# Attention scores stored block behind block, and the maximum over them taken in two halves, in a two-layer graph kernel

## The chip, the cores and the metric

The kernel runs on one core of one Trainium2 chip. The time is that of the device, in microseconds (us). The kernel before took 818.03 us, the median of 3 runs that lay between 816.57 and 819.36 us. Engines are named as in the profile: PE is TensorE's matmul, PEld its weight load, DVE is VectorE, ACT is ScalarE, POOL is GpSimd and SP is SyncE.

## The reference, cut to what matters

A graph has 3125 nodes with 128 features and 103,125 edges. The first layer adds to each node a weighted sum over its neighbours. The second layer, where the change lies, is attention over the edges that arrive at each node:

```
h = relu(layernorm(x))
q, k, v = h @ Wq + bq, h @ Wk + bk, h @ Wv + bv
logits = sum(q[dst] * k[src], axis=-1) / sqrt(128)
m = segment_max(logits, dst);  ex = exp(logits - m[dst])
alpha = ex / segment_sum(ex, dst)[dst]
x = x + elu(segment_sum(alpha * v[src], dst) + h @ Ws + bs)
```

## The kernel before

The kernel turns edges into dense tables. Nodes are laid out in NT = 25 tiles of P = 128. The first stage (up to about 70 us) sorts out windows of edges; the second (to about 472 us) builds, for each tile of destination nodes, a table `gt` of the logarithms of edge counts and the weighted sums of the first layer; the third (to about 508 us) makes keys `kT`, queries `qT`, values `vals` and the skip term. The fourth is attention, one step for each of the 25 tiles t of destinations, written in queues that run in order, one for each engine.

In a step, a tile of 128 destinations is scored against all 25 source blocks of 128 nodes. The score table `sm[:, v, :]` has the source node within its block on the partitions; along a partition lie all blocks h and, in each, the 128 destinations d. A ring of RING = 4 such tables is in use (v is t modulo 4), and as many tables `gl_sb` of edge logarithms, which SP loads four tiles ahead. The blocks are taken in NSG = 4 groups given by `SG`: 6, 6, 6 and 8 blocks, the last of which holds 7 real blocks and one of padding (NTP = 26), filled once by POOL with a very low number. Groups 0 and 2 share one pair of PSUM banks, groups 1 and 3 the other, so group 2 can be scored only after group 0 is read out, and group 0 of tile t+1 only after group 2 of tile t.

For one group the work goes round the engines: ACT seeds the banks from `gl_sb` (`seed`, L668, a large number where there is no edge; it waits until DVE has read the group that was there); PE adds the scores (`scores`, L1259, one float32 matmul for each block, which the profile shows as two records); DVE subtracts them from `gl_sb` into `sm` (`mask`, L994). After the fourth group DVE takes the maximum over the 25 blocks and the pad for each partition and destination (L1033), PE turns the result (L1280), DVE reduces it to one maximum for each destination and puts it on a diagonal (L1010, L1013), PE spreads it with a matmul against ones (L1286), ACT copies it to `mbc` (L710), POOL subtracts it from the four groups of `sm` (`subtract_max`, L493), ACT takes the exponential of each (L717), and PE multiplies by the values and a column of ones (`values`, L1270, 129 columns, again two records for each block, with `sm` as the stationary operand). Then DVE and ACT normalise and apply the skip term and the ELU (L1017 to L1026, L691 to L696), and POOL adds the residual.

The steps overlap. In step t PE does, in this order: turn the maximum of t-1 (L1280); scores of t, group 2; spread the maximum of t-1 (L1286); scores of t, group 3; values of t-2, groups 0 and 1; scores of t+1, groups 0 and 1; values of t-2, groups 2 and 3. DVE does: mask 0, mask 1; L1010, L1013 for t-1; L1017, L1020 for t-3; mask 2; L1026 for t-3; mask 3; the maximum. ACT does: seeds 2 and 3 of t; `mbc` of t-1; exponential 0 of t-1, seed 0 of t+1, exponential 1, seed 1 of t+1, exponential 2, the ELU of t-3, exponential 3.

The layout of `sm` before is paired: two neighbouring blocks i = 0, 1 are interleaved word by word, so word 2d + i of pair k belongs to block 2k + i and destination d. The function `twos` gives that view. `mask` writes with a step of 2 words, L1033 reads for each d the two words of a pair, hops 256 words to the next pair, and so on 13 times, and `values` loads its weights with a step of 2 words.

Of the kernel before, what the change touches and what calls it, by code (L numbers as in the profile page):

```python
# [79 lines left out]

SG = [(0, 6), (6, 6), (12, 6), (18, 8)]
NTP = NT + 1
NSG = len(SG)
# [3 lines left out]
STEPS = NT + 3  # L87
assert sum(n for _, n in SG) == NTP and all(n % 2 == 0 for _, n in SG) and NSG % 2 == 0 and LOOP_TO < NT

# [8 lines left out]
def build_gnn(nc, x, dst, dst_next, dst_far, dst_rows, samples, src, edge_weight, ids, consts, slow_iota,  # L98
              ws_t, wn_t, wq, wk, wv, wskip, b_s, b_n, bq, bk, bv, b_skip, out):
    outer = ExitStack()  # L100
    with outer:
# [3 lines left out]
        def sb(stack, name, shape, dt=F32):  # L105
            return stack.enter_context(nc.sbuf_tensor(name, shape, dt))
# [10 lines left out]
        def ps(i):  # L117
            return bank[i // 2][:, i % 2, :]
# [162 lines left out]
        s4 = ExitStack()  # L281
        mx = sb(s4, "mx", [P, P])
        mcol = sb(s4, "mcol", [P, 1])
        diag = sb(s4, "diag", [P, P])
# [5 lines left out]
        res = sb(s4, "res", [P, 2, D])  # L290
        sm = sb(s4, "sm", [P, RING, NTP * P])
        gl_sb = sb(s4, "gl_sb", [P, RING, NTP * P])
        s4.close()
        s34.close()
        gl = [sem(f"gl{k}") for k in range(RING)]
        seeded, primed, pad_ready = sem("seeded"), sem("primed"), sem("pad_ready")
        s_ready, masked, mx_ready, mt_ready, m_ready, dg_ready, mb_ready, mbc_ready = (
# [12 lines left out]

        def twos(v, a, n):

            return sm[:, v, a * P:(a + n) * P].rearrange("p (k d i) -> p k d i", d=P, i=2)

# [119 lines left out]
        def _(pool):  # L434
# [47 lines left out]
            pool.memset(vals[:, :, D:D + 1], 1.0)  # L482
            pool.memset(gl_sb[:, :, NT * P:NTP * P], -FLOOR).then_inc(pad_ready, 1)
            for d in range(1, NC):
# [3 lines left out]
            def subtract_max(t, v):  # L488
                pool.wait_ge(mbc_ready, 1 + t + 1)
                for a, n in SG:  # L490
                    part = twos(v, a, n)
                    top = mbc[:, v % 2, :].unsqueeze(1).unsqueeze(3).to_broadcast([P, n // 2, P, 2])
                    pool.tensor_tensor(part, part, top, ALU.subtract).then_inc(sub_done, 1)  # L493
# [240 lines left out]
        def _(dve):  # L734
# [256 lines left out]
            def mask(t, v, g):  # L991
                a, n = SG[g]
                dve.wait_ge(s_ready, t * NSG + g + 1)
                V.tensor_tensor(twos(v, a, n).rearrange("p k d i -> p k i d"),  # L994
                                gl_sb[:, v, a * P:(a + n) * P].rearrange("p (k i d) -> p k i d", d=P, i=2),
                                score_bank(g)[:, 0:n * P].rearrange("p (k i d) -> p k i d", d=P, i=2),
                                ALU.subtract).then_inc(masked, 1)

            def dve_step(t, v, turn):
# [18 lines left out]
                if three:  # L1018
                    dve.wait_ge(rd_ready, 2 * (t - 3) + 1)
                    V.reciprocal(rden[:, u3, :], rden[:, u3, :]).then_inc(rd_ready, 1)  # L1020
                if now:
                    mask(t, v, 2)
                if three:
# [7 lines left out]
                if now:  # L1031
                    dve.wait_ge(masked, 2 + (t + 1) * NSG)
                    V.tensor_reduce(mx[:], twos(v, 0, NTP).rearrange("p k d i -> p d k i"), AXY, ALU.max).then_inc(mx_ready, 1)  # L1033

            dve.wait_ge(pad_ready, 1)
            for t in range(LOOP_FROM):
# [9 lines left out]
        def _(pe):  # L1046
# [216 lines left out]
            def values(t, v, g):  # L1263
# [4 lines left out]
                for h in range(a, min(a + n, NT)):  # L1268
                    weights = twos(v, h - h % 2, 2).rearrange("p k d i -> p (k d) i")[:, :, h % 2]
                    ins = T.matmul(ps(4 + v % 2)[:, 0:D + 1], weights, vals[:, h, :], start=h == 0,  # L1270
                                   stop=h == NT - 1)
# [85 lines left out]
```

## Time and profile before

| | us |
|---|---|
| median of 3 runs | 818.03 |
| the profiled execution | 822.52 |
| its span, first to last instruction | 820.6 |
| PE busy, whole span | 735.8 |
| DVE busy | 618.0 |
| ACT busy | 526.4 |
| POOL busy | 253.9 |

Busy time is that in which at least one instruction of the engine was running. The granted TensorE clock was 0.99 of full speed over the span. The table is over the whole kernel; only the last 310 us, the attention, are touched by the change, so the shares of that stretch matter and are among the rows below.

### The profile page before, as it was taken

How to read it: one execution, taken by the hardware profiler on the slowest of the kernel's cores; microseconds unless marked ns; L12 is line 12 of the kernel's file. 1: busy time of each engine (PE TensorE's matmuls, PEld its weight loads, DVE VectorE, ACT ScalarE, POOL GpSimd, SP SyncE). 2: the span in 40 equal slices, each digit the busy share in tenths (PEclk: the TensorE clock that was granted, in tenths of full speed). 3: DMA queues.
4: the chain of work that ended last, by engine and by line, in shares of the span. 5: the costliest groups of instructions: out<-in, count | busy, mean ns of one | idle time of the engine just before them, and what ended most of it. 6: DMA issues, size and time to landing. Idle time of an engine off the chain costs nothing.

```text
span 820.6 us, 24234 instructions
## 1 busy us (share of the span) xinstructions
PE 735.8 (90%) x9625; PEld 719.5 (88%) x9625; DVE 618.0 (75%) x778; ACT 526.4 (64%) x1056; POOL 253.9 (31%) x206
## 2 busy tenths in 40 slices
PE   0147999999999999999999688699999999999997
PEld 0147999999999999999999666699999999999996
DVE  6767779889889889889885653776777677767771
ACT  4949857667667767767766234566676666667654
POOL 4636000000000000000000141366676667666766
PEclk9999999999999999999999979999999999999999
DMA  9831223212212212212312170404334433443300
GB/s 263 256 103 77 88 81 133 111 80 120 120 80 120 120 80 117 122 80 110 130 80 115 51 320 1 161 2 168 120 133 163 165 114 136 166 161 106 148 8 12
DMA packets 17667, 96.79 MB, mean 118 GB/s; under 512 B 2482, under 2 KB 8860, under 8 KB 11100
## 3 DMA queue, kind: packets, MB, share of 16 engines
q1 hardware_dynamic: 14572, 90.08, 28.9%
q0 software_dynamic: 3056, 6.17, 2.9%
q8 instruction: 27, 0.44, 0.2%
q14 instruction: 12, 0.10, 0.0%
HBM read 51.62 MB, written 44.63 MB: 117 GB/s over the span
## 4 chain that ended last, share of the span: by engine, by line
PE 83%; ACT 6%; DVE 5%; issue 2%; POOL 1%; another core or an unknown queue 1%; DMA 1%; POOLq 1%; PEld 0%; PEldq 0%; ACTq 0%; DVEq 0%
PE bank L1270 18%; PE bank L1119 17%; PE bank L1259 16%; PE bank L1136 9%; PE bank L1134 9%; PE bank L1101 8%; PE bank L1225 1%; PE bank L1230 1%; ACT kT L554 1%; ACT wst L607 1%; DVE oh_key L914 1%; ACT gst L605 1%; PE bank L1087 1%; DVE junk L751 1%
## 5 line engine op out<-in xcount | busy, mean ns | idle before, releaser
L493 POOL TENSOR_TENSOR sm<-sm,mbc 128x768 f32<-128x768 f32 x100 | 174.5, 1777 | 115.4 <-ACT mbc L710 115.4
L1134 PE MATMUL bank<-oh_key,oh_lo 128*128 128x100 bf16 x1600 | 170.6, 208 | 8.0 <-ACT wst L607 6.7
L1136 PE MATMUL bank<-oh_key,oh_lo 128*128 128x50 bf16 x3200 | 170.9, 187 | 0.0
L1134 PEld LDWEIGHTS bank<-oh_key,oh_lo 128*128 128x128 bf16 x1600 | 155.7, 97 | 10.5 <-ACT wst L607 8.6
L1136 PEld LDWEIGHTS bank<-oh_key,oh_lo 128*128 128x128 bf16 x3200 | 163.8, 97 | 0.9
L1259 PE MATMUL bank<-qT,kT 128*128 (+1 forms) x1250 | 154.1, 277 | 6.8 <-ACT bank L668 6.8
L1270 PE MATMUL bank<-vals,sm 128*128 128x129 f32 x1250 | 154.8, 281 | 0.0
L1259 PEld LDWEIGHTS bank<-qT,kT 128*128 128x128 f32 x1250 | 147.1, 194 | 8.2 <-ACT bank L668 7.0
L1270 PEld LDWEIGHTS bank<-vals,sm 128*128 128x128 f32 x1250 | 150.9, 196 | 0.0
L914 DVE TENSOR_TENSOR oh_key<-oh_key,xt 128x1600 bf16<-128x1600 bf16 x150 | 141.9, 1001 | 0.0
L605 ACT ACTIVATE gst<-bank,tiny_col 128x400 f32<-128x400 f32 x200 | 122.4, 612 | 23.6 <-PE bank L1136 20.4
L476 POOL TENSOR_TENSOR xn<-xs,ln_c 128x640 f32<-128x640 f32 x5 | 7.8, 1564 | 405.1 <-DVE ln_c L874 405.1
L1119 PE MATMUL bank<-hv,qT 128*128 (+1 forms) x650 | 128.3, 285 | 2.0 <-DVE kT L844 2.0
L717 ACT ACTIVATE sm<-sm 128x768 f32<-128x768 f32 x100 | 89.9, 899 | 58.5 <-POOL sm L493 55.5
L994 DVE TENSOR_TENSOR sm<-gl_sb,bank 128x768 f32<-128x768 f32 x100 | 100.0, 1020 | 32.6 <-PE bank L1259 32.6
L1119 PE MATMUL bank<-hv,wsb 128*128 (+1 forms) x600 | 116.0, 275 | 0.0
L909 DVE TENSOR_TENSOR oh_lo<-xt,lo_tab 128x4096 bf16<-128x4096 bf16 x50 | 114.2, 2285 | 0.0
L607 ACT COPY wst<-bank 128x400 f32<-128x400 f32 x200 | 100.7, 504 | 0.0
L1119 PEld LDWEIGHTS bank<-hv,qT 128*128 128x128 f32 x650 | 96.7, 191 | 2.5 <-DVE kT L844 2.3
L1033 DVE TENSOR_REDUCE mx<-sm 128x128 f32<-128x3328 f32 x25 | 90.5, 3620 | 0.9
L1119 PEld LDWEIGHTS bank<-hv,wsb 128*128 128x128 f32 x600 | 91.1, 192 | 0.0
L844 DVE TENSOR_TENSOR kT<-kT,bank 128x512 f32<-128x512 f32 (+1 forms) x84 | 52.7, 628 | 49.3 <-PE bank L1119 48.3
(122 smaller groups left out, 808.3 us busy)
## 6 DMA issues: line engine op xcount, KB each, us to landing
gt<-gst SPq DMA_DIRECT2D x25, 1600.0 KB, 5.5
gl_sb<-gt SPq DMA_DIRECT2D x25, 1600.0 KB, 6.7
records<-rec SPq DMA_DIRECT2D x1, 2015.0 KB
out<-res SPq DMA_DIRECT2D x24, 64.0 KB, 1.5
src_i<-in_src SPq DMA_DIRECT2D x1, 403.0 KB, 6.2
w_in<-in_edge_weight SPq DMA_DIRECT2D x1, 403.0 KB, 6.6
dst_i<-in_dst SPq DMA_DIRECT2D x1, 403.0 KB, 7.1
dstn_i<-in_dst_next SPq DMA_DIRECT2D x1, 403.0 KB, 7.2
```

Of the source, the lines that this page charges most:

```text
L493: pool.tensor_tensor(part, part, top, ALU.subtract).then_inc(sub_done, 1)
L605: nc.scalar.activation(place, counts, ACT.Ln, bias=tiny_col[:, 0:1], scale=EULER).then_inc(evacs, 1)
L607: nc.scalar.copy(sums, cells[:, :, KEYS:2 * KEYS]).then_inc(evacs, 1)
L909: V.tensor_tensor(oh_lo[:, u, :, :, :], along(F_LO, P), table(lo_tab, P), ALU.is_equal).then_inc(onehot, 1)
L914: V.tensor_tensor(block(1 + w), block(0), along(F_W + w, KEYS), ALU.mult).then_inc(onehot, 1)
L994: V.tensor_tensor(twos(v, a, n).rearrange("p k d i -> p k i d"), gl_sb[:, v, a * P:(a + n) * P].rearrange("p (k i d) -> p k i d", d=P, i=2 ...
L1033: V.tensor_reduce(mx[:], twos(v, 0, NTP).rearrange("p k d i -> p d k i"), AXY, ALU.max).then_inc(mx_ready, 1)
L1119: ins = T.matmul(to, wsb[w][:, cols], hv[:, bass.ds(s, 1), :].rearrange("p t f -> p (t f)"), start=n == 0 and not first, stop=n == len(par ...
L1134: T.matmul(cells, lo, oh_key[:, u, m, 0:2 * KEYS, i], start=True, stop=False, skip_group_check=True)
L1136: ins = T.matmul(cells[:, KEYS:2 * KEYS], lo, oh_key[:, u, m, (1 + w) * KEYS:(2 + w) * KEYS, i], start=False, stop=w == 2, skip_group_chec ...
L1259: ins = T.matmul(score_bank(g)[:, j * P:(j + 1) * P], kT[:, (a + j) * P:(a + j + 1) * P], qT[:, bass.ds(t * P, P)], start=False, stop=True ...
L1270: ins = T.matmul(ps(4 + v % 2)[:, 0:D + 1], weights, vals[:, h, :], start=h == 0, stop=h == NT - 1)
```

## The change

`sm` loses the pairing: block h lies whole behind block h-1, `sm[:, v, h*128 + d]`. The pad block goes, with its fill and the wait for it. The groups become 7, 6, 6 and 6 blocks. `mask` writes contiguously, `subtract_max` has the same elements in a view of blocks, and `values` loads contiguous weights. The one maximum over 26 blocks becomes one over the 13 blocks of groups 0 and 1, issued on DVE ahead of mask 2; one over the 12 blocks of groups 2 and 3, after mask 3; and an elementwise maximum of the two results. Both halves read, for each destination d, one word of each block with a hop of 128 words between them.

```
-SG = [(0, 6), (6, 6), (12, 6), (18, 8)]
-NTP = NT + 1
+SG = [(0, 7), (7, 6), (13, 6), (19, 6)]
+HALF = SG[2][0]
...
-        sm = sb(s4, "sm", [P, RING, NTP * P])
-        gl_sb = sb(s4, "gl_sb", [P, RING, NTP * P])
+        mx_half = sb(s4, "mx_half", [P, 2, P])
+        sm = sb(s4, "sm", [P, RING, NT * P])
+        gl_sb = sb(s4, "gl_sb", [P, RING, NT * P])
...
-            return sm[:, v, a * P:(a + n) * P].rearrange("p (k d i) -> p k d i", d=P, i=2)
+            return sm[:, v, a * P:(a + n) * P].rearrange("p (h d) -> p h d", d=P)
...
-            pool.memset(gl_sb[:, :, NT * P:NTP * P], -FLOOR).then_inc(pad_ready, 1)
...
-                    part = twos(v, a, n)
-                    top = mbc[:, v % 2, :].unsqueeze(1).unsqueeze(3).to_broadcast([P, n // 2, P, 2])
+                    part = blocks(v, a, n)
+                    top = mbc[:, v % 2:v % 2 + 1, :].to_broadcast([P, n, P])
...
-                V.tensor_tensor(twos(v, a, n).rearrange("p k d i -> p k i d"),
-                                gl_sb[:, v, a * P:(a + n) * P].rearrange("p (k i d) -> p k i d", d=P, i=2),
-                                score_bank(g)[:, 0:n * P].rearrange("p (k i d) -> p k i d", d=P, i=2),
+                V.tensor_tensor(sm[:, v, a * P:(a + n) * P], gl_sb[:, v, a * P:(a + n) * P], score_bank(g)[:, 0:n * P],
                                 ALU.subtract).then_inc(masked, 1)
+            def half_max(t, v, k):
+                a, n = (HALF, NT - HALF) if k else (0, HALF)
+                dve.wait_ge(masked, 2 + t * NSG + 2 * k + 2)
+                V.tensor_reduce(mx_half[:, k, :], blocks(v, a, n).rearrange("p h d -> p d h"), AX, ALU.max).then_inc(mx_part, 1)
...
                     V.reciprocal(rden[:, u3, :], rden[:, u3, :]).then_inc(rd_ready, 1)
                 if now:
+                    half_max(t, v, 0)
                     mask(t, v, 2)
...
                 if now:
-                    dve.wait_ge(masked, 2 + (t + 1) * NSG)
-                    V.tensor_reduce(mx[:], twos(v, 0, NTP).rearrange("p k d i -> p d k i"), AXY, ALU.max).then_inc(mx_ready, 1)
+                    half_max(t, v, 1)
+                    dve.wait_ge(mx_part, 2 * t + 2)
+                    V.tensor_tensor(mx[:], mx_half[:, 0, :], mx_half[:, 1, :], ALU.max).then_inc(mx_ready, 1)
...
-                    weights = twos(v, h - h % 2, 2).rearrange("p k d i -> p (k d) i")[:, :, h % 2]
-                    ins = T.matmul(ps(4 + v % 2)[:, 0:D + 1], weights, vals[:, h, :], start=h == 0,
+                    ins = T.matmul(ps(4 + v % 2)[:, 0:D + 1], sm[:, v, h * P:(h + 1) * P], vals[:, h, :], start=h == 0,
```

## Rows read from the trace of the kernel before

**Rows 1.** Busy by engine, 21 steady steps: PE, PEld, DVE, ACT, POOL, clock, DMA.
```profile
545.19:793.13 247.94, 247.94 (x2165) 247.94 (x2164) 180.66 (x210) 162.11 (x273) 165.03 (x126) 1.00 0.37 131
```

**Rows 2.** Timeline of PE over one steady step: start us, length us, line, count.
```profile
651.14 0.27 PE L1280 MATMUL bank<-ident,mx 128*128 128x128 f32 x1
...
657.21 2.84 PE L1259 MATMUL bank<-qT,kT 128*128 x24
659.88 3.23 PE L1270 MATMUL bank<-vals,sm 128*128 128x129 f32 x26
662.95 0.27 PE L1280 MATMUL bank<-ident,mx 128*128 128x128 f32 x1
```

**Rows 3.** Timeline of DVE, the same step; in brackets idle time and its releaser.
```profile
651.45 0.29 DVE L1010 TENSOR_REDUCE mcol<-bank 128x1 f32<-128x128 f32 x1 [2.07 <-PE bank L1280]
...
652.17 0.16 DVE L1020 RECIPROCAL rden<-rden 128x1 f32<-128x1 f32 x1
652.79 0.95 DVE L994 TENSOR_TENSOR sm<-gl_sb,bank 128x768 f32<-128x768 f32 x1 [0.46 <-PE bank L1259]
653.66 0.35 DVE L1026 SCALAR_TENSOR_TENSOR pre<-bank,rden,hT 128x128 f32<-128x128 f32 x1
654.58 1.22 DVE L994 TENSOR_TENSOR sm<-gl_sb,bank 128x1024 f32<-128x1024 f32 x1 [0.57 <-PE bank L1259]
655.84 3.62 DVE L1033 TENSOR_REDUCE mx<-sm 128x128 f32<-128x3328 f32 x1
```

**Rows 4.** Timeline of POOL and ACT, the same step.
```profile
653.36 6.97 POOL L493 TENSOR_TENSOR sm<-sm,mbc 128x768 f32<-128x768 f32 x4 [3.69 <-ACT mbc L710]
...
655.04 0.85 ACT L717 ACTIVATE sm<-sm 128x768 f32<-128x768 f32 x1 [1.76 <-POOL sm L493]
655.79 0.80 ACT L668 ACTIVATE bank<-gl_sb 128x768 f32<-128x768 f32 x1
```

**Rows 5.** Groups by form, attention stage: busy us, mean ns of one, idle before.
```profile
L493 POOL TENSOR_TENSOR sm<-sm,mbc 128x768 f32<-128x768 f32 x75 | 121.9, 1654 | 115.4 <-ACT mbc L710 115.4
...
L493 POOL TENSOR_TENSOR sm<-sm,mbc 128x1024 f32<-128x1024 f32 x25 | 53.6, 2146 | 0.0
...
L717 ACT ACTIVATE sm<-sm 128x1024 f32<-128x1024 f32 x25 | 26.5, 1060 | 9.7 <-POOL sm L493 9.7
L668 ACT ACTIVATE bank<-gl_sb 128x896 f32<-128x896 f32 x25 | 22.6, 904 | 0.7 <-DVE sm L994 0.6
```

**Rows 6.** Groups by form, DVE, first 70 us.
```profile
L827 DVE TENSOR_TENSOR xin<-win,nid 128x384 bf16<-128x384 f32 x3 | 2.5, 849 | 0.0
L785 DVE TENSOR_TENSOR rec<-rest,part_b 128x806 f32<-128x806 f32 x1 | 1.6, 1627 | 0.0
L827 DVE TENSOR_TENSOR xin<-win,nid 128x256 bf16<-128x256 f32 x2 | 1.3, 632 | 0.8 <-issue 0.8
L780 DVE TENSOR_TENSOR rest<-w_in,part_b 128x806 f32<-128x806 f32 x1 | 1.0, 1000 | 0.0
```

**Rows 7.** Timeline of PE, a run of transposes in the second stage.
```profile
303.37 1.06 PE L1101 MATMUL bank<-ident,wst 128*128 128x128 f32 x8
```

**Rows 8.** Timeline of all engines, the first attention step.
```profile
510.18 0.96 DVE L994 TENSOR_TENSOR sm<-gl_sb,bank 128x768 f32<-128x768 f32 x1 [2.79 <-PE bank L1259]
511.23 0.81 ACT L668 ACTIVATE bank<-gl_sb 128x768 f32<-128x768 f32 x1 [2.17 <-DVE sm L994]
...
512.09 3.18 PE L1259 MATMUL bank<-qT,kT 128*128 128x128 f32 x26 [0.71 <-ACT bank L668]
...
513.74 0.95 DVE L994 TENSOR_TENSOR sm<-gl_sb,bank 128x768 f32<-128x768 f32 x1 [1.36 <-PE bank L1259]
...
516.56 3.62 DVE L1033 TENSOR_REDUCE mx<-sm 128x128 f32<-128x3328 f32 x1
```

**Rows 9.** Timeline of all engines, around the last maximum.
```profile
796.26 1.23 DVE L994 TENSOR_TENSOR sm<-gl_sb,bank 128x1024 f32<-128x1024 f32 x1 [0.57 <-PE bank L1259]
...
801.95 0.27 PE L1280 MATMUL bank<-ident,mx 128*128 128x128 f32 x1
```

More of the change, by code:

```diff
@@ L87 @@
 STEPS = NT + 3
-assert sum(n for _, n in SG) == NTP and all(n % 2 == 0 for _, n in SG) and NSG % 2 == 0 and LOOP_TO < NT
+assert sum(n for _, n in SG) == NT and NSG % 2 == 0 and LOOP_TO < NT
 TG = [(a, min(4, NT - a)) for a in range(0, NT, 4)]
@@ L295, in build_gnn @@
         gl = [sem(f"gl{k}") for k in range(RING)]
-        seeded, primed, pad_ready = sem("seeded"), sem("primed"), sem("pad_ready")
+        seeded, primed, mx_part = sem("seeded"), sem("primed"), sem("mx_part")
         s_ready, masked, mx_ready, mt_ready, m_ready, dg_ready, mb_ready, mbc_ready = (
@@ L309, in score_bank, with blocks @@
             return bank[g % 2][:].rearrange("p a b -> p (a b)")
-        def twos(v, a, n):
-            return sm[:, v, a * P:(a + n) * P].rearrange("p (k d i) -> p k d i", d=P, i=2)
+        def blocks(v, a, n):
+            return sm[:, v, a * P:(a + n) * P].rearrange("p (h d) -> p h d", d=P)
         def live(t):
@@ L1031, in dve_step @@
                 if now:
-                    dve.wait_ge(masked, 2 + (t + 1) * NSG)
-                    V.tensor_reduce(mx[:], twos(v, 0, NTP).rearrange("p k d i -> p d k i"), AXY, ALU.max).then_inc(mx_ready, 1)
-            dve.wait_ge(pad_ready, 1)
+                    half_max(t, v, 1)
+                    dve.wait_ge(mx_part, 2 * t + 2)
+                    V.tensor_tensor(mx[:], mx_half[:, 0, :], mx_half[:, 1, :], ALU.max).then_inc(mx_ready, 1)
             for t in range(LOOP_FROM):
```

## The prediction

> **What bounds the kernel now.** I read the page first for the whole span: PE is busy 735.8 of 820.6 us. I then cut the attention stage out with busy time by stretch [rows 1]: over 247.94 us, PE is busy for 247.94, at a granted clock of 1.00 (the 2.4 GHz level), while DVE is busy for 180.7, ACT 162.1 and POOL 165.0. That stretch is 21 steps of 247.94 / 21 = 11.81 us, as the distance of two L1280 in the timeline also says [rows 2]. So a step ends when PE has gone through its 50 score records, 50 value records and 3 others; nothing that only makes DVE, ACT or POOL faster shortens it, and whatever makes PE wait lengthens it one for one.
>
> The timelines of the other engines say how far each is from making PE wait. I count from the start of a step, T = 651.14 [rows 2]. DVE ends its maximum at 655.84 + 3.62 = T+8.32 [rows 3], and PE asks for it at T+11.81: 3.5 us of slack. The near one is another wait. PE starts the scores of t+1, group 0, at 657.21 = T+6.07 [rows 2]. These need seed 0, which runs on ACT from 655.79 to 656.59 [rows 4], and that needs mask 2, over at 652.79 + 0.95 = T+2.60 [rows 3]. Today ACT is at that seed late only because exponential 0 stands ahead of it.
>
> **The change part by part.** First the pitch of PE. Groups 7, 6, 6, 6 make the same 25 blocks. Scores come every (659.88 - 657.21) / 24 = 0.111 us, values every (662.95 - 659.88) / 26 = 0.118 [rows 2]. Is the difference of 0.0065 the step of 2 words in the weights, or the 129th column and what comes with it? Rows on both sides: transposes whose stationary operand is read every 25th word come at (1.06 - 0.28) / 7 = 0.112 [rows 7], so a hop in the stationary operand by itself costs nothing there; that is nearest in kind, and I take 0. The other end is 50 x 0.0065 = 0.32 us gained a step.
>
> Masks: 768 elements take 0.95 and 1024 take 1.22 [rows 3], so 128 elements take 0.135, already the slope of one element each 1.05 ns; contiguous writes have no more to give. Mask 0 becomes 1.09, mask 3 0.95. The pad's fill ran once, beside other work: 0.
>
> Next the maximum. Now 3328 elements take 3.62 us [rows 3], 1.04 ns each and 0.15 fixed; the hops of 256 words between pairs are free. In the change every element hops. The trace before has no such reduction. Bounds: below, the present 1.04 ns. Above, the DVE rows of the first 70 us with a hop each element: L827 reads every fifth word, 384 in 849 ns and 256 in 632; less 150 fixed that is 1.82 and 1.88 ns (by their difference alone 1.70); L785 writes every fifth word, 806 in 1627 ns against 1000 for the contiguous L780, 0.78 ns more each, 1.82 in all [rows 6]. I take 1.81, the long read. The first half is then 0.15 + 1664 x 0.00181 = 3.17 us, the second 0.15 + 1536 x 0.00181 = 2.93, and the joining operation 0.29 like other 128-column ones (L1010) [rows 3]: 6.39 for 3.62.
>
> [...]
>
> Second, where it stands. The first half sits on DVE ahead of mask 2, behind L1020, which starts at 652.17 = T+1.03 [rows 3]; the half starts at T+1.11, and queued behind it are mask 2, L1026 and mask 3. Neighbours on DVE overlap by 0.08 (652.79 + 0.95 against 653.66). Mask 2 runs from 1.11 + 3.17 - 0.08 = T+4.20 to T+5.15, 2.55 later than today. ACT takes up a seed 0.09 after the mask (510.18 + 0.96 to 511.23) and PE its scores 0.05 after the seed, with about 0.11 more for the first weight load that then isn't hidden [rows 8]. A seed of 896 is 0.90 [rows 5]. So the scores of t+1 start at 5.15 + 0.09 + 0.90 + 0.16 = T+6.30. PE is free for them at T+6.07, plus 0.01 (two score records fewer, two value records more ahead of them). It waits 0.22 us in each step. The rest of the step is unchanged, 11.81 becomes 12.03, and 21 steps give +4.6 us.
>
> Beside it stands the way through POOL and ACT to the same seed: the subtraction of 7 blocks is (2146 - 1654) / 2 = 246 ns longer [rows 5], so exponential 0 starts at 655.04 + 0.25 [rows 4]; the seed follows 0.75 later and 0.11 more for the longer exponential (1060 against 850 for two blocks [rows 4, 5]), at T+5.01. That is 0.23 ahead of DVE's way; with a fast reduction this one would be last, and scores could start at 5.01 + 0.90 + 0.16 = T+6.07: no wait, but no slack either.
>
> The rest of DVE's step: L1026 and mask 3 to T+6.27, second half from 6.31 to 9.24, the joining from 9.28 to 9.57. PE wants it at T+12: hidden, at less cover. Masks 0 and 1 follow to T+11.45, 0.9 before the next L1010. Seed 1 waits for mask 3 and exponential 1 and ends near T+7.6, before its scores at 7.9. SP's loads wait for mask 3 and have whole steps to spare; POOL's and SP's queues are moved past nothing.
>
> Two ends don't repeat. In the first step mask 2 starts at 513.74 with DVE idle 1.36 before it [rows 8]. The first half begins there near 512.6 and ends at 515.8; mask 2, mask 3 (0.95 each), 2.93 and 0.29 bring the maximum to 520.8 instead of 516.56 + 3.62 = 520.2, and the next step's seed, with no values yet to cover it, loses about as much again: +0.9 (0.3 to 1.3). In the last step T is 793.13 - 0.31 = 792.82 (the L1010 that ends rows 1's stretch), so the last maximum is there at 792.82 + 9.57 = 802.4 where PE now turns it at 801.95 [rows 9], and everything after waits for it: +0.5.
>
> **Sum.** 4.6 + 0.9 + 0.5 = +6.0 us, made against the profiled 822.52 (span 820.6 and 1.9 around it): 828.5. The profiled execution is 0.5% above the median of 818.03; nothing of the sum hangs on that, so I add the same 6.0 to the median: 824.0.
>
> **Rivals.**
>
> A dearer hop. If a hop of 128 words costs twice the extra of five words, it is 1.04 + 2 x 0.77 = 2.6 ns. Then DVE itself is the bound: its fixed parts in a step (from L1010 to the first half 0.80; mask 2, L1026, mask 3 and handovers 2.1; the two 0.15 less overlaps; joining 0.2; masks 0 and 1 1.9) are 5.3, and with 3200 elements the step is 5.3 + 8.3 = 13.6 us: +1.8 x 21 = 38 us, about 857. It decides from 2.04 ns on. For it: a longer hop. Against it: no row here shows more than 1.88, and the pair hop of 256 words is free. [...]
>
> The hop is free. L1033 hops between pairs at no cost, and only two-input operations show the penalty in rows 6. The halves cost 1.88 and 1.75, DVE gets slack, and PE waits by POOL's way for nothing: 818.0, no change. It decides below 1.70 ns, where the wait is gone.
>
> The paired weights are what slows the values. Then every step gives back 0.32. With the hop as I forecast, PE is at the scores 0.17 sooner, but they start at T+6.30 all the same; only the 24 records behind give 0.16, so a step is +0.07, the ends +1.4 less 150 x 0.0065 = 1.0: +1.9 us, 820, within what can't be told.
>
> The other side: paired weights and a free hop together. This is one mechanism, the interleaving taken off PE, with price 0.32 a step, and it decides if the values' pitch drops to 0.112. POOL's way holds the scores at T+6.07, so only 0.16 of it is kept: 3.4 us, and 1.0 in the last 150 records: 813.6, faster. For it: the pitch difference of 0.0065, of which one more column explains little. Against it: rows 7, and rows 6 speak against the free hop.
>
> That the change doesn't do what it says: if L1020 were late for want of values of t-3, the half would be too; rows 3 show it at T+1.03, with no idle time, so no.
>
> **How the numbers follow.** My forecast, 0.50; dearer hop, 0.12; free hop, 0.16; paired weights with a dear hop, 0.14; both gone, 0.08. A measurement of this kernel tells about 0.3%, 2.5 us, from no change. Slower: the forecast but for its low edge (by 1.70 ns it gives +1.7 us), the dearer hop, and a little of the third: 0.58. Same: 0.28. Faster: 0.14. The likeliest case's own range is 819.7 to 827. To hold the time 8 times in 10 the range goes down to 815, which takes in the free hop, and up to 834; the dearer hop is left out above.
>
> **What would show it.** In the profile after: the 13-block reduction near 3.17 us and the 12-block one near 2.93; mask 2 without idle time before it, starting 4.2 us after L1280; idle time of PE at L1259, released by L668, about 0.2 us and 21 times; a step of 12.03; L1270's pitch still 0.118. The prediction is wrong if the halves are near 1.9 or above 3.6 us, or if L1270's pitch falls to 0.112.

## The result, and the profile after

The changed kernel takes 823.24 us (median of 6 runs, 820.73 to 824.61) against 817.30 for the kernel before (6 runs, 816.42 to 820.20): 5.9 us more, a ratio of 1.0063 with a 95% interval of 1.0044 to 1.0082. The forecast was 824.0, slower. The direction and the size came out; the way to them did so only in part. That the total came so near is luck: the steps cost less than forecast and the ends more, and within a step two errors cancel in part.

The profiled execution took 824.57 us. I first cut out the same 21 steps. The columns are as in [rows 1], from the third L1283 (the former L1280) to the twenty-fourth; [rows 1] begins and ends 0.31 us later in its step, at L1010.

```profile
542.40:793.30 250.90, 247.18 (x2165) 243.19 (x2164) 236.61 (x252) 163.17 (x274) 175.61 (x126) 1.00 0.37 130
```

PE isn't saturated any more: 3.7 of 250.9 us are idle, and PEld, in which a wait shows better, idles for 7.7. DVE has gone from 180.7 to 236.6 us. A step is 250.9 / 21 = 11.95 us. Next the costliest groups by form, attention stage (busy us, mean ns, idle before):

```profile
L1273 PE MATMUL bank<-vals,sm 128*128 128x129 f32 x1250 | 148.8, 276 | 0.0
L1263 PEld LDWEIGHTS bank<-qT,kT 128*128 128x128 f32 x1250 | 148.4, 195 | 18.4 <-ACT bank L668 9.7 <-issue 8.7
...
L493 POOL TENSOR_TENSOR sm<-sm,mbc 128x768 f32<-128x768 f32 x75 | 134.7, 1829 | 0.0
...
L1000 DVE TENSOR_REDUCE mx_half<-sm 128x128 f32<-128x1664 f32 x25 | 76.8, 3072 | 0.0
L1000 DVE TENSOR_REDUCE mx_half<-sm 128x128 f32<-128x1536 f32 x25 | 73.0, 2918 | 0.9
...
L493 POOL TENSOR_TENSOR sm<-sm,mbc 128x896 f32<-128x896 f32 x25 | 52.3, 2092 | 110.4 <-ACT mbc L710 110.4
...
L1038 DVE TENSOR_TENSOR mx<-mx_half 128x128 f32<-128x128 f32 x25 | 16.9, 674 | 0.9
```

The halves are 3.07 and 2.92 us (forecast 3.17 and 2.93). Two rows nobody asked for: POOL takes 1.83 us for the 768 elements that took 1.65 [rows 5], and the joining takes 0.67 where 0.29 was summed. The timeline of one steady step (T = 650.09, the L1283 that begins it) has the rest, all engines:

```profile
650.09 0.27 PE L1283 MATMUL bank<-ident,mx 128*128 128x128 f32 x1
...
652.31 7.44 POOL L493 TENSOR_TENSOR sm<-sm,mbc 128x896 f32<-128x896 f32 x4 [3.39 <-ACT mbc L710]
...
654.21 0.94 DVE L994 TENSOR_TENSOR sm<-gl_sb,bank 128x768 f32<-128x768 f32 x1
654.43 0.95 ACT L717 ACTIVATE sm<-sm 128x896 f32<-128x896 f32 x1 [2.20 <-POOL sm L493]
...
655.29 0.90 ACT L668 ACTIVATE bank<-gl_sb 128x896 f32<-128x896 f32 x1
...
656.33 2.98 PEld L1263 LDWEIGHTS bank<-qT,kT 128*128 128x128 f32 x26 [0.35 <-issue]
656.33 3.16 PE L1263 MATMUL bank<-qT,kT 128*128 x26 [0.16 <-ACT bank L668]
...
659.27 0.63 DVE L1038 TENSOR_TENSOR mx<-mx_half 128x128 f32<-128x128 f32 x1
659.33 2.84 PE L1273 MATMUL bank<-vals,sm 128*128 128x129 f32 x24
...
662.01 0.27 PE L1283 MATMUL bank<-ident,mx 128*128 128x128 f32 x1
```

Three things are to be seen. The 24 value records go from 659.33 to 662.01: 2.68 / 24 = 0.112 us each, not 0.118 as in [rows 2]. PE stands before the scores of group 0, for seed 0, as forecast. But seed 0 starts at 655.29, the moment exponential 0 gives ACT free; mask 2 had been done since 655.15, 0.14 before. What came last was POOL's way, not mask 2, though not by much: a seed follows its mask by some 0.04 us where it waits for nothing else (the run with the hop and POOL's old view, below), so 0.10 of the 0.14 counts. This step takes 11.92 us. Three in four do; the fourth, in which seed 0 comes some 0.1 us later, takes 12.0 to 12.1, and the mean is 11.95.

The wait is sized by the step: 103 records at 0.1115 would be 11.48, so PE waits 0.46 us in each on the mean, where I had 0.22 on top of 11.81.

The three stretches of attention, from the first instruction of the third stage (L977 on DVE, at 472.72 and 466.67 us) in both profiles:

| | before | after | forecast |
|---|---|---|---|
| to the third L1010 (L1013) | 72.5 | 76.0 | +0.9 |
| 21 steps | 247.9 | 250.9 | +4.6 |
| from there to the end | 27.5 | 29.2 | +0.5 |
| sum | 347.9 | 356.1 | +6.0 |

The sum is 8.2 us, more than the 5.9 of the medians. What lies ahead of attention differs by 6 us between profiles, even of one and the same design, so I compare stretches, not spans. Those 6 us go with the chip: the runs below that were made on the chip where the kernel before takes 818.3 us have 466.3 to 466.9 there, like the profile of after; those made on the three chips where it takes 824.2 to 824.6 have 471.8 to 472.9, like the profile of before. What it is in the chip, no run here shows. The profile of before, with 822.52 us, is thus to be held against 824 and not 818: it is of an execution some 1.7 to 2.1 us faster than the median, while that of after lies 1.3 above its own. Together that covers the 2.3 us between 8.2 and 5.9.

So the ends cost 5.2 us by the two profiles and, by the medians, 5.9 less the 3.0 of the steps, 2.9; forecast were 1.4. Busy time by stretch, three of after and then three of before: its first and third lie at the same place in the program as those of after, its second is the one in which its clock was low (columns as above; the granted clock is the number behind the brackets):

```profile
509.00:515.00 6.00, 3.80 (x21) 3.61 (x20) 5.66 (x5) 1.68 (x2) 0.00 (x0) 0.74 0.40 130
527.00:533.00 6.00, 4.29 (x22) 4.11 (x23) 5.96 (x7) 2.70 (x4) 0.23 (x1) 0.72 0.27 113
804.00:810.00 6.00, 5.80 (x37) 5.80 (x38) 0.73 (x4) 2.06 (x3) 4.93 (x3) 0.72 0.04 11
```

```profile
515.00:521.00 6.00, 3.81 (x28) 3.04 (x26) 5.66 (x4) 1.41 (x2) 0.00 (x0) 1.00 0.55 190
527.00:533.00 6.00, 4.68 (x25) 4.44 (x25) 5.07 (x3) 4.62 (x6) 4.24 (x3) 0.72 0.76 273
804.00:810.00 6.00, 6.00 (x53) 6.00 (x52) 0.42 (x3) 2.84 (x6) 6.00 (x4) 1.00 0.01 3
```

In each of the three stretches of after the granted clock is 0.72 to 0.74 on the mean, a mixture of the 2.4 GHz and the 1.2 GHz level; before has one such stretch. Each costs at most 6 x 0.28 = 1.7 us; in the last one PE is busy nearly throughout and does 37 records in 6 us, where before does 53. They follow idle time of PE: in after PE had stood 2.2 us before 511.78 for a seed that stood behind the first half maximum, and 1.8 us around the last L1283 and L1289. Not all idle time was followed by one: PE also stood 3.04 us before 523.44, and its clock was 1.00 from 523 to 529. From the timeline of after:

```profile
506.82 3.03 DVE L1000 TENSOR_REDUCE mx_half<-sm 128x128 f32<-128x1664 f32 x1
...
509.77 1.81 DVE L994 TENSOR_TENSOR sm<-gl_sb,bank 128x768 f32<-128x768 f32 x2
510.81 1.68 ACT L668 ACTIVATE bank<-gl_sb 128x896 f32<-128x896 f32 x2 [3.11 <-DVE sm L994]
...
511.78 4.80 PE L1263 MATMUL bank<-qT,kT 128*128 128x128 f32 x26 [2.20 <-ACT bank L668]
514.43 0.29 DVE L1038 TENSOR_TENSOR mx<-mx_half 128x128 f32<-128x128 f32 x1
...
516.42 0.27 PE L1283 MATMUL bank<-ident,mx 128*128 128x128 f32 x1
...
803.17 0.33 PE L1283 MATMUL bank<-ident,mx 128*128 128x128 f32 x1 [1.11 <-DVE mx L1038]
...
804.20 0.49 PE L1289 MATMUL bank<-diag,ones 128*128 128x128 f32 x2 [0.71 <-DVE diag L1016]
```

The first maximum is there at 514.43 + 0.29 = 514.72, 48.05 us after the start of the third stage, against 47.46 before: the 0.6 later that I had forecast. But PE turns it only at 516.42, 2.2 us later than before, since its 26 records from 511.78 take 4.80 us where 26 take 3.18 at full clock [rows 8]; that is 1.6 of the 2.2.

Two such stretches more are up to 3.4 of the 8.2 us. How many an execution has isn't set by the kernel alone. On one chip (that of the late-join run below) the kernel before took 814.8 to 816.5 us in the nine executions with a mean granted clock of 0.990 or 0.991, and 818.1 to 820.3 in the fourteen with 0.984 to 0.988. So what one profile shows at the two ends is good to a few microseconds only, while the steady steps, at a clock of 1.00, are not touched by it.

### The profile page after: what moved, and what is told of

Same layout as the page of the kernel before. It is cut to its first block, busy times and chain, and to the rows that moved or that the text cites. A ratio compares the mean times of both kernels' runs of the same rounds, so it can differ in the third digit from the quotient of the medians.

```text
span 822.8 us, 24313 instructions
## 1 busy us (share of the span) xinstructions
PE 737.6 (90%) x9625; PEld 717.1 (87%) x9625; DVE 686.0 (83%) x828; ACT 527.1 (64%) x1056; POOL 267.8 (33%) x205
## 4 chain that ended last, share of the span: by engine, by line
PE 51%; POOL 20%; issue 14%; ACT 6%; DVE 6%; POOLq 1%; DMA 1%; PEld 0%; PEldq 0%; ACTq 0%; DVEq 0%
POOL sm L493 18%; PE bank L1123 17%; PE bank L1140 9%; PE bank L1138 9%; PE bank L1105 8%; PE bank L1273 2%; PE bank L1229 1%; PE bank L1263 1%; POOL res L499 1%; PE bank L1234 1%; ACT kT L554 1%; ACT wst L607 1%; ACT gst L605 1%; PE bank L1091 1%; DVE junk L751 1%
## 5 line engine op out<-in xcount | busy, mean ns | idle before, releaser
L493 POOL TENSOR_TENSOR sm<-sm,mbc 128x896 f32<-128x896 f32 (+1 forms) x100 | 186.0, 1894 | 110.4 <-ACT mbc L710 110.4
L1263 PE MATMUL bank<-qT,kT 128*128 (+1 forms) x1250 | 157.6, 281 | 13.1 <-ACT bank L668 13.0
L1000 DVE TENSOR_REDUCE mx_half<-sm 128x128 f32<-128x1664 f32 (+1 forms) x50 | 149.8, 2995 | 0.9
L1273 PE MATMUL bank<-vals,sm 128*128 128x129 f32 x1250 | 148.8, 276 | 0.0
L1273 PEld LDWEIGHTS bank<-vals,sm 128*128 128x128 f32 x1250 | 145.0, 193 | 0.0
L717 ACT ACTIVATE sm<-sm 128x896 f32<-128x896 f32 (+1 forms) x100 | 87.1, 871 | 65.2 <-POOL sm L493 64.6
L994 DVE TENSOR_TENSOR sm<-gl_sb,bank 128x896 f32<-128x896 f32 (+1 forms) x100 | 95.9, 977 | 5.3 <-PE bank L1263 4.9
L668 ACT ACTIVATE bank<-gl_sb 128x896 f32<-128x896 f32 (+1 forms) x100 | 83.1, 833 | 20.4 <-DVE sm L994 17.9
```

What stands on the lines that cost most here:

```text
L994: V.tensor_tensor(sm[:, v, a * P:(a + n) * P], gl_sb[:, v, a * P:(a + n) * P], score_bank(g)[:, 0:n * P], ALU.subtract).then_inc(masked, 1)
L1000: V.tensor_reduce(mx_half[:, k, :], blocks(v, a, n).rearrange("p h d -> p d h"), AX, ALU.max).then_inc(mx_part, 1)
L1263: ins = T.matmul(score_bank(g)[:, j * P:(j + 1) * P], kT[:, (a + j) * P:(a + j + 1) * P], qT[:, bass.ds(t * P, P)], start=False, stop=True ...
L1273: ins = T.matmul(ps(4 + v % 2)[:, 0:D + 1], sm[:, v, h * P:(h + 1) * P], vals[:, h, :], start=h == 0, stop=h == NT - 1)
```

## Experiments

Twelve kernels, each timed beside the kernel before on the same chip. Step, start and end are read as in the table above, from each profile; for the ends, what was just said of single profiles holds. Ratios are to the kernel before, with 95% intervals. The edits shown are cut to the lines that matter; the runs whose text speaks of a tiny scale also have `scale=2.0 ** -100` in the exponential. What holds for before and after: step 11.81 and 11.95, start 72.5 and 76.0, end 27.5 and 29.2.

**Is it the paired weights that slow the values?**

```
-                    weights = twos(v, h - h % 2, 2).rearrange("p k d i -> p (k d) i")[:, :, h % 2]
+                    weights = sm[:, v, h * P:(h + 1) * P]
```

> The kernel before, in which the value matmuls load 128 neighbouring words as weights (those of block h as if the table were not paired) and not every second word; the products are therefore of mixed-up scores, nothing else differs. Theory A, the step of 2 words in the weights slows the value matmuls: a value record comes every 0.1115 us and not 0.118, no wait of PE appears (seed 0 ends at T+5.45 and PE is there at T+5.92), a steady step is 11.48 us and not 11.81, the time some 8 us lower, 809. Rival, the pitch belongs to the 129th column or to where the values lie, and fell in the changed kernel for another reason: pitch 0.118, step 11.81, 817.

Measured: ratio 0.9916 (0.9892 to 0.9939), step 11.51, start 71.8, end 26.4. From its timeline of PE:

```profile
655.55 3.07 PE L1270 MATMUL bank<-vals,sm 128*128 128x129 f32 x26
658.46 0.27 PE L1280 MATMUL bank<-ident,mx 128*128 128x128 f32 x1
```

The 26 records take 2.91 us, 0.112 each: nothing but the step of the weights was changed, and 0.30 us a step went. Theory A stands. The reverse, the changed kernel with paired weights:

```
-                    ins = T.matmul(ps(4 + v % 2)[:, 0:D + 1], sm[:, v, h * P:(h + 1) * P], vals[:, h, :], start=h == 0,
+                    b = min(h - (h - a) % 2, a + n - 2)
+                    weights = sm[:, v, b * P:(b + 2) * P].rearrange("p (d i) -> p d i", i=2)[:, :, (h - a) % 2]
+                    ins = T.matmul(ps(4 + v % 2)[:, 0:D + 1], weights, vals[:, h, :], start=h == 0,
```

> The changed kernel in which the value matmuls load every second word of two neighbouring blocks as weights, as the kernel before did (the products are of mixed-up scores). This is the kernel that the prediction summed. A value record comes every 0.118 us again. Scores of group 0 start at T+6.24, where POOL's way puts them, as in the changed kernel; only the 24 value records behind them are dearer: a step of 11.95 + 0.16 = 12.10 us, 3.3 us more in the steady steps, the ends 0.5 to 1 more, the time 0.5% above that of the changed kernel on the same chip. Rival, the pitch of the values comes from elsewhere: step 11.95.

Measured: ratio 1.0082 (1.0057 to 1.0106), step 12.09, start 76.2, end 28.1. The step is the expected one to 0.01; the total, whose interval reaches over that of the changed kernel, can't tell 0.2% from the expected 0.5%. Its values, from the timeline of PE:

```profile
660.34 2.99 PE L1275 MATMUL bank<-vals,sm 128*128 128x129 f32 x24
663.17 0.27 PE L1285 MATMUL bank<-ident,mx 128*128 128x128 f32 x1
```

2.83 / 24 = 0.118. So the step that I had summed as 12.03 is 12.09 in a kernel with the pitch that I had assumed.

**Why is POOL slower?**

```
-                    part = twos(v, a, n)
-                    top = mbc[:, v % 2, :].unsqueeze(1).unsqueeze(3).to_broadcast([P, n // 2, P, 2])
+                    part = sm[:, v, a * P:(a + n) * P].rearrange("p (h d) -> p h d", d=P)
+                    top = mbc[:, v % 2:v % 2 + 1, :].to_broadcast([P, n, P])
```

> The kernel before, in which POOL's subtraction of the maximum takes the view of the changed kernel (blocks one behind the other, the row of maxima repeated for each block), which pairs wrong maxima with the scores; the exponential has a tiny scale so that its results stay finite. Theory B, it is this view that makes POOL slower: 768 elements take 1.83 us and not 1.65, with the paired reduction on DVE as before; exponential 0 starts 0.18 later, still no wait of PE, time 817 to 818. Rival, POOL is slowed by DVE's hopping reads at the same time: 1.65 us stays.

Measured: ratio 1.0041 (1.0026 to 1.0056), step 11.98, start 73.2, end 27.3. Groups by form:

```profile
L493 POOL TENSOR_TENSOR sm<-sm,mbc 128x768 f32<-128x768 f32 x75 | 134.5, 1821 | 102.4 <-ACT mbc L710 102.4
...
L493 POOL TENSOR_TENSOR sm<-sm,mbc 128x1024 f32<-128x1024 f32 x25 | 59.4, 2378 | 0.0
```

Theory B stands: with the paired maximum on DVE, POOL is slower all the same, by the view alone. Where two neighbouring elements share a word of the second operand, an element costs (2146 - 1654) / 256 = 1.92 ns [rows 5], else (2378 - 1821) / 256 = 2.18. (The changed kernel's own rows give (2092 - 1829) / 128 = 2.05.) The total missed: I had looked at seed 0 only. The timeline of ACT and PE in this run:

```profile
656.90 0.84 ACT L717 ACTIVATE sm<-sm 128x768 f32<-128x768 f32 x1 [1.92 <-POOL sm L493]
657.65 0.80 ACT L668 ACTIVATE bank<-gl_sb 128x768 f32<-128x768 f32 x1
658.68 0.84 ACT L717 ACTIVATE sm<-sm 128x768 f32<-128x768 f32 x1 [0.24 <-POOL sm L493]
...
658.90 1.28 PE L1259 MATMUL bank<-qT,kT 128*128 x10
659.43 0.80 ACT L668 ACTIVATE bank<-gl_sb 128x768 f32<-128x768 f32 x1
```

ACT waits 0.24 us for POOL's second subtraction, and seed 1 behind it ends at 660.23; PE, through with group 0 after 12 records at 658.90 + 1.34 = 660.24, can't take it up before 660.23 + 0.16. That is about 0.15 of the 0.17 us a step. There is a second narrow place, seed 1.

**What does the hop cost in time, and which way binds?**

```
-  blocks(v, a, n).rearrange("p h d -> p d h")
+  sm[:, v, a * P:(a + n) * P].rearrange("p (d h) -> p d h", d=P)
```

> The changed kernel, in which both half maxima read the same number of words without a hop (for each destination 13 or 12 neighbouring words, which are the wrong ones; the exponential has a tiny scale for the same reason as before). The halves take 1.88 and 1.75 us and mask 2 starts near T+2.9. Theory C, in the changed kernel seed 0 waits for POOL's first subtraction and exponential 0, and mask 2 comes only just before them: exponential 0 still starts near T+4.3, PE still waits some 0.2 us, a steady step is 11.9 and not 11.95; the time falls by 1 us in the steady steps and by 2 to 3 at the two ends, to 820. Rival, the prediction's own step (mask 2 sets the start, POOL is only slowed by DVE's hops): POOL back at 1.9 for the first group, step 11.78 or less, 817.

Measured: ratio 0.9987 (0.9971 to 1.0003), step 11.93, start 71.5, end 26.4. From its timeline:

```profile
652.70 1.89 DVE L1000 TENSOR_REDUCE mx_half<-sm 128x128 f32<-128x1664 f32 x1
...
655.90 0.95 ACT L717 ACTIVATE sm<-sm 128x896 f32<-128x896 f32 x1 [2.19 <-POOL sm L493]
...
656.76 0.90 ACT L668 ACTIVATE bank<-gl_sb 128x896 f32<-128x896 f32 x1
...
657.80 3.16 PE L1263 MATMUL bank<-qT,kT 128*128 x26 [0.15 <-ACT bank L668]
```

Without the hop the first half takes 1.89 us for 3.07, and the steady step gains 0.02 us. Theory C stands: exponential 0 and seed 0 start where POOL lets them, and PE's wait is there still. Without the hop the two ends lose their cost, though: 4.5 us at the start and 2.8 at the end against the profile of after. The ratio fell by 0.0076 against the changed kernel, some 6 us (good to 2), of which the steps are 0.3, and more than the 3 us expected. The hop's price is paid at the ends.

With POOL's old kind of view as well:

```
-  part = blocks(v, a, n)
+  part = sm[:, v, a * P:(a + n) * P].rearrange("p (h e i) -> p h e i", e=P // 2, i=2)
-  top = mbc[:, v % 2:v % 2 + 1, :].to_broadcast([P, n, P])
+  top = mbc[:, v % 2, 0:P // 2].unsqueeze(1).unsqueeze(3).to_broadcast([P, n, P // 2, 2])
```

> As the run before, and besides POOL's subtraction with a view like that of the kernel before (two neighbouring words share a maximum, the wrong one). Theories B and C together: POOL's first subtraction takes 1.90 us and not 2.10, exponential 0 starts near T+4.15, PE waits some 0.1 us or less, a step is 11.7 to 11.78, the time 2.5 to 4 us below that of the run before. If C is wrong, no difference to the run before.

Measured: ratio 0.9926 (0.9907 to 0.9946), step 11.74, start 70.7, end 26.2. As expected: 0.20 us a step, by POOL's view, once mask 2 is early; the time fell by some 5 us against the run before, more than the 4 expected. And that view alone, the hop kept (the edit just shown, without that of the halves):

> The changed kernel with only POOL's subtraction taken back to a view like that of the kernel before (two neighbouring words share a maximum, the wrong one; the exponential has a tiny scale so that its results stay finite). POOL's first subtraction takes 1.90 us and not 2.10, so exponential 0 and with it ACT are ready for seed 0 at T+5.01. Mask 2 still ends near T+5.06 and seed 0 can't start before T+5.15: by my sum mask 2 is then the last, and only 0.05 us a step is gained, 1 us in all and 0.5 at the ends, 821.7. Rival, mask 2 has slack and only POOL's way counts: 0.19 us a step, 4 us, 819.

Measured: ratio 0.9993 (0.9979 to 1.0007), step 11.84, start 72.5, end 27.2. Half of what it gives without the hop: 0.11 us a step, twice my 0.05, since seed 0 then follows mask 2 by 0.04 and not 0.09. So mask 2, as the prediction had it, is the next to bind, just behind POOL's way. The total came out below both expectations: 0.0070 less than the ratio of the changed kernel, some 5.7 us, of which the steps are 2.2. At the two ends this run, with the full hop, cost 3.5 and 2.0 us less than the profile of after. Its profiled execution is the fastest of its twelve and has a clock of 1.00 from 508 to 538 us, where after has two low stretches worth up to 3.4 us. So POOL's view seems to be paid for at the ends too, beside the hop; what of it is POOL's time and what the clock's, these runs don't separate.

**One maximum, behind mask 3** (the layout alone, the halves undone):

```
-                    half_max(t, v, 0)
...
-                    half_max(t, v, 1)
-                    dve.wait_ge(mx_part, 2 * t + 2)
-                    V.tensor_tensor(mx[:], mx_half[:, 0, :], mx_half[:, 1, :], ALU.max).then_inc(mx_ready, 1)
+                    dve.wait_ge(masked, 2 + (t + 1) * NSG)
+                    V.tensor_reduce(mx[:], blocks(v, 0, NT).rearrange("p h d -> p d h"), AX, ALU.max).then_inc(mx_ready, 1)
```

> The changed kernel's layout and groups, but one maximum over all 25 blocks behind mask 3, nothing between masks 1 and 2; the full computation. The one reduction of 3200 words with a hop each takes 0.15 + 3200 x 0.00178 = 5.85 us. Mask 2 is done at T+2.6, mask 3 at T+4.2, the maximum at T+10.1. Seed 0 is left to POOL's way (T+5.2): PE waits some 0.2 us there, as in the changed kernel; mask 0 of the next step ends at 11.15, its seed 2 at 12.0, which PE wants at 11.8: another 0.3. Step 12.1 to 12.3, 826 to 831. Rival (only the sum of DVE's work counts, which is smaller without the joining): 822 or less.

Measured: ratio 1.0090 (1.0074 to 1.0107), step 12.02, start 77.1, end 28.0. The reduction takes 5.88 us (5.85 expected); the step is 0.1 better than expected, and the ratio is below the expected 1.011 to 1.017. The halves are worth 0.07 us a step to the block layout: they make part of the maximum early.

**Towards a better kernel.** The first partial maximum over group 0 alone:

```
-SG = [(0, 7), (7, 6), (13, 6), (19, 6)]
-HALF = SG[2][0]
+SG = [(0, 6), (6, 6), (12, 6), (18, 7)]
+HALF = SG[1][0]
...
-                dve.wait_ge(masked, 2 + t * NSG + 2 * k + 2)
+                dve.wait_ge(masked, 2 + t * NSG + 3 * k + 1)
```

> The changed kernel with groups 6, 6, 6, 7 and the first partial maximum over group 0 alone (6 blocks), the second over the other 19; the full computation. The first takes 1.5 us, so mask 2 ends near T+3.5; POOL's first subtraction has 6 blocks and takes 1.83, exponential 0 is 0.85 and seed 0 can start at T+4.83 and PE its scores at T+5.8, before it is free at 5.9. No wait there, a step of 103 x 0.1115 = 11.48 us. The second maximum takes 4.5 and ends near T+9.3, the joining waits for POOL's last subtraction until T+9.8, mask 0 of the next step ends at 10.7 and its seed 2 at 11.6, which PE wants at 11.6: here 0 to 0.15 us may be lost. 810 to 813 against 817.3 before. Rival: DVE, with 11.2 us of work a step, can't keep 11.48, and the step stays at 11.9 or so: 820.

Measured: ratio 1.0017 (1.0002 to 1.0031), step 11.85, start 76.1, end 27.5. Missed: 810 to 813 us were expected, where the kernel before takes 817.3. The reason is the second narrow place, met in the run with POOL's view of blocks. The timeline:

```profile
661.07 0.84 ACT L717 ACTIVATE sm<-sm 128x768 f32<-128x768 f32 x1 [0.24 <-POOL sm L493]
661.82 0.80 ACT L668 ACTIVATE bank<-gl_sb 128x768 f32<-128x768 f32 x1
662.67 1.41 PEld L1263 LDWEIGHTS bank<-qT,kT 128*128 128x128 f32 x12 [0.23 <-ACT bank L668]
```

The wait has moved from group 0 to group 1: PE waits for seed 1, that for exponential 1, and that for POOL. Next, in the same kernel, another way of joining:

```
-        mx_half = sb(s4, "mx_half", [P, 2, P])
+        mx_half = sb(s4, "mx_half", [P, P, 2])
...
-                V.tensor_reduce(mx_half[:, k, :], ...
+                V.tensor_reduce(mx_half[:, :, k], ...
-                    V.tensor_tensor(mx[:], mx_half[:, 0, :], mx_half[:, 1, :], ALU.max)
+                    V.tensor_reduce(mx[:], mx_half[:], AX, ALU.max)
```

> As the run before, but the two partial maxima are written side by side and joined by a reduction with one input in place of an elementwise operation with two; the full computation. Theory D, the elementwise operation with two SBUF inputs (0.62 us median, 0.29 in the first step, when POOL is idle) waits for POOL's running subtraction: a reduction of 256 words takes 0.42 us whatever POOL does, mask 0 and seed 2 come 0.3 earlier, and the wait at seed 2 goes: up to 3 us faster than the run before. Rival, the 0.62 is something else: the joining stays above 0.6.

Measured: ratio 1.0018 (1.0004 to 1.0031), step 11.85, start 76.4, end 27.4 (one of its twelve executions took 4128 us, for a reason that isn't known). The joining takes 0.42 us every time (0.54 on the mean in the run before), as theory D has it, and it brings nothing, since it isn't what PE waits for.

On ACT the seeds go ahead of the exponentials:

```
+                    if g < 2:
+                        next_seed(g)
                     if live(t - 1):
                         act.wait_ge(sub_done, 2 * NSG + s * NSG + g + 1)
                         part = sm[:, w, a * P:(a + n) * P]
                         nc.scalar.activation(part, part, ACT.Exp).then_inc(exp_done, 1)
-                    if g < 2:
-                        next_seed(g)
```

> The kernel with the first group alone (groups 6, 6, 6, 7), and on ACT seed 0 ahead of exponential 0 and seed 1 ahead of exponential 1; the full computation. Theory E, in that kernel (step 11.85) PE waits 0.3 us for seed 1, which waits on ACT behind exponential 1 for POOL's second subtraction: with the seeds first, they wait for the masks alone, seed 0 starts near T+3.6 and seed 1 near T+4.9, and PE's waits before the scores of groups 0 and 1 are gone. What is late next is DVE: its second maximum, the joining and mask 0 end near T+10.8, seed 2 of the next step near T+11.65, where PE wants it at T+11.6: a step of 11.5 to 11.6, and 1.5 to 2.5% less time than the kernel before. Rival, DVE's own sum of work (some 11.3 us and its handovers) keeps the step at 11.85.

Measured: ratio 1.0005 (0.9987 to 1.0022), step 11.65, start 75.5, end 27.6. The waits before groups 0 and 1 are gone and the step is 0.2 us shorter, so theory E stands for the step; 0.05 to 0.15 more remain than expected. The total, where I had promised 1.5 to 2.5%, shows nothing. I had left the start out of it.

The joining goes behind mask 0 of the next step:

```
+                if before:
+                    dve.wait_ge(mx_part, 2 * t)
+                    V.tensor_tensor(mx[:], mx_half[:, 0, :], mx_half[:, 1, :], ALU.max).then_inc(mx_ready, 1)
                 if now:
                     mask(t, v, 1)
...
                     half_max(t, v, 1)
-                    dve.wait_ge(mx_part, 2 * t + 2)
-                    V.tensor_tensor(mx[:], mx_half[:, 0, :], mx_half[:, 1, :], ALU.max).then_inc(mx_ready, 1)
```

> As the run before, and the joining of the two partial maxima issued behind mask 0 of the next step, not ahead of it; the full computation. POOL's last subtraction is over by then, so the joining takes 0.3 us and not 0.54; mask 0 ends near T+10.2, seed 2 has 0.5 us of slack, the maximum is there at T+10.5 where PE wants it at T+11.4. Step 11.48 to 11.52, bound by PE alone: up to 2 us less than the run before. Rival, mask 1 or the turned maximum becomes late instead: the same as the run before or more.

Measured: ratio 0.9959 (0.9944 to 0.9973), step 11.50, start 77.9, end 27.5. From its timeline:

```profile
657.17 0.94 DVE L994 TENSOR_TENSOR sm<-gl_sb,bank 128x768 f32<-128x768 f32 x1
657.60 0.46 POOL L499 TENSOR_TENSOR res<-pos,xs 128x128 f32<-128x128 f32 x1
...
658.03 0.28 DVE L1011 TENSOR_TENSOR mx<-mx_half 128x128 f32<-128x128 f32 x1
```

The joining takes 0.28 us once POOL's subtractions are over. The step is PE's own 11.5 again, this kernel computes everything and is 0.4% faster than the kernel before: 21 x 0.31 = 6.4 us are gained in the steps. By the profiles 5.5 are given back at the start, where PE's clock is at half for two stretches; by the medians, 3.6 us apart, it is 2.8 at both ends together. Busy time and clock of the second such stretch, in the run before and in this one (columns as above):

```profile
529.00:535.00 6.00, 6.00 (x41) 6.00 (x41) 3.68 (x5) 2.60 (x5) 3.45 (x2) 0.72 0.01 3
530.00:536.00 6.00, 5.77 (x28) 5.76 (x28) 3.17 (x5) 2.37 (x5) 2.03 (x2) 0.50 0.01 3
```

The last run tried to win the start back: the joining of tiles 0 and 1 at once, in place of the joining just shown.

```
+                def join(k):
+                    dve.wait_ge(mx_part, 2 * k)
+                    V.tensor_tensor(mx[:], mx_half[:, 0, :], mx_half[:, 1, :], ALU.max).then_inc(mx_ready, 1)
+
+                if before and not (isinstance(t, int) and t <= 2):
+                    join(t)
...
                     half_max(t, v, 1)
+                    if isinstance(t, int) and t < 2:
+                        join(t + 1)
```

> The kernel with the seeds first and the late joining, except that the joining of tiles 0 and 1 is issued at once behind their second maximum; the full computation. Theory F, what keeps that kernel from more than 0.4% is the filling of the pipeline: from the start of the third stage to the third L1010 it took 77.9 us against 72.5 in the kernel before and 75.5 with the early joining, since mask 0 of the next tile, ahead of the joining, waits for its scores while PE stands still and its clock falls to half. With the early joining for two tiles that stretch is 75.5 again, the steady step stays at 11.50 us, and the time is 2 to 2.5 us below the kernel with late joining throughout: 0.7% below the kernel before. Rival, the filling is bound by PE's clock whatever DVE's order: no difference to it, 0.4%.

Measured: ratio 0.9963 (0.9947 to 0.9979), step 11.50, start 78.0, end 27.5. Theory F falls: neither the ratio nor the start has moved. Its premise was weak, too. The start of 75.5 us is that of the fastest of twelve executions of the seeds-first kernel (816.19, median 817.81), the 77.9 that of the slowest of twelve with the late joining (815.61, median 814.73). The medians are 3.1 us apart, which is what the steps give, 21 x 0.147: they show no difference at the ends. Within the profiles the clock is enough to make the 2.5 us: in two stretches of 6 us at the start it is 0.72 in the one and 0.50 in the other, up to 2.6 us. Why it was low for longer there stays open.

## Why the prediction was right, point by point

- **What bounds, and the near wait.** Right. The scores of t+1, group 0, were the place where PE came to stand, and seed 0 the cause; their weight load begins at T+6.24, where 6.30 less the 0.11 of that load, 6.19, was forecast.
- **The hop.** Right: 3.07 and 2.92 us for 3.17 and 2.93, that is 1.75 and 1.80 ns an element with 0.15 fixed, near the rows of every fifth word [rows 6] from which I took 1.81.
- **Which way came last.** Wrong. I had "the subtraction of 7 blocks is 246 ns longer" and POOL's way 0.23 ahead of mask 2. POOL's first subtraction is 2.09 us and not 1.90, because of the view that I had passed over as "the same elements"; exponential 0 comes 0.19 later, and seed 0 starts 0.14 behind the end of mask 2. By luck it starts nearly where mask 2 was to let it, at T+5.20 for T+5.24. The run with flat halves shows it: 1.2 us less for the first half, 0.02 us less for the step.
- **The pitch of the values.** Wrong. "A hop in the stationary operand by itself costs nothing there; I take 0" failed: the step of 2 words cost 0.0065 us a record, as the run with plain weights and the one with paired weights show from both sides. The transposes [rows 7] were no fair row: another kind of operation, one record for each where a matmul has two. Why their hop of 25 words is free and this one of 2 is not, no run here shows. The 129th column, to which I left the difference, is still there at 0.112. By its own last sentence the prediction was wrong here: a pitch of 0.112 is among the signs that it named. The two errors have opposite signs: I had 11.81 + 0.22 = 12.03, it is 11.48 + 0.46 = 11.95, so the steps gave +3.0 us for my +4.6.
- **The rival "paired weights with a dear hop"** is the mechanism that came true in the steps, with its price too low: it gave +0.07 a step for the measured 0.14. POOL's 0.19 is not what it lacked, since seed 0 starts where it was to start, for another reason. In the steady step PE's first weight load comes 0.14 behind the seed's end (655.29 + 0.90 to 656.33), where I took 0.05 from [rows 8]: less the 0.04 that the seed is early, that is 0.05. And every fourth step is some 0.1 longer, 0.03 on the mean. What makes the 0.14, no run here shows.
- **The ends.** Right in sign, mis-sized: 0.9 and 0.5 us were 3.6 and 1.7 in the profiles, and by the medians 2.9 in all for 1.4. The late maxima are there (the first is ready 0.6 us later, as forecast; the last L1283 stands 1.1 us for L1038, at T+9.87 instead of 9.13), but I had left out that PE, after standing, works on at the 1.2 GHz level for a while; the trace before had such a stretch, at 527 to 533, which I had passed over in the mean of 0.99. "TensorE: Matmul & The Clock Gate" of the Trainium skill, section "Part 1: The HAM clock gate", says that an idle TensorE drops to 1.2 GHz and gets 2.4 back only after being busy again; the stretches of after agree: each low one follows idle time and ends while PE works, though the idle 3.04 us before 523.44 were followed by none.
- **The joining.** Wrong in size, 0.67 for 0.29, without consequence in the steady step. It takes 0.29 when POOL is idle and otherwise ends some 0.15 us behind POOL's running subtraction (659.90 for 659.75 in the step shown). "GPSIMD Engine Reference" of the Trainium skill, section "Key points", names DVE operations with two SBUF inputs as contending with POOL; the runs agree: 1.16 us on the mean with the flat halves, where it begins earlier in POOL's work, 0.42 constant as a one-input reduction.

So: slower by what was said, and for the reason said in so far as PE waits for seed 0 in every step. That the size came out is luck: two errors in the steady step cancelled in part, and an underestimate at the ends made up the difference.

## What to carry to other kernels

When an edit is a change of layout, price the new view for every engine that reads or writes the tensor, not only for the one it is made for: here DVE got 2.7 us more work a step, POOL 0.5, and PE 0.32 less. When one wait is forecast, list the other arrivals at the same place and the same place in the next group: both decided here. And where a kernel fills and drains its pipeline, idle time of PE may be paid twice, the second time in clock. Since one execution has more of that than another, take what a change costs at the ends from medians less the steady steps, not from one profile against one.

## What the runs showed of the hardware

- A float32 weight load with a step of 2 words spaces two-record matmuls at 0.118 us for 0.112 with neighbouring words (the runs with plain and with paired weights).
- POOL's subtraction of 768 elements takes 1.83 us, and 1.65 in the views where two neighbouring elements share a word of the second operand; 1024 take 2.38 and 2.15.
- A DVE maximum over words 128 apart costs 1.75 to 1.80 ns an element, 1.04 over neighbouring words or over pairs with hops of 256 between them.
- A DVE operation of 128 columns with two inputs in SBUF takes 0.29 us while POOL is idle, and 0.67 on the mean beside POOL's subtractions; as a one-input reduction of 256 words it takes 0.42 throughout.
- After idle time of PE its granted clock was lower for a while: 0.72 to 0.74 over 6 us, in three stretches of the changed kernel's profile and in one of the profile before, up to 1.7 us each. Executions of one kernel on one chip differ in it, by some 2 to 4 us of time.
